# A graph attention layer's edge stage: queries two chunks ahead, values turned and copied first, row loads on another queue

## The reference, cut to what matters

```python
q = (embeds[rows] @ qW).reshape(e, HEADS, dh)          # rows = src, HEADS = 4, dh = 24
k = (embeds[cols] @ kW).reshape(e, HEADS, dh)          # cols = dst
v = (embeds[cols] @ vW).reshape(e, HEADS, dh)
scores = jnp.clip(jnp.einsum('ehd,ehd->eh', q, k), -10.0, 10.0)
exp_s = jnp.exp(scores)
norms = jax.ops.segment_sum(exp_s, rows, num_segments=nvar)[rows]
w = exp_s / (norms + 1e-08)
res = jax.ops.segment_sum(w[:, :, None] * v, rows, num_segments=nvar).reshape(nvar, d)
```

## Time and profile before

| | |
|---|---|
| median of 3 runs | 12264.51 us (12244.3 to 12269.51) |
| profiled execution, its own time | 12250.97 us |
| its span, first to last instruction | 12249.1 us |
| TensorE busy | 8795.0 us (72%) |
| VectorE busy | 5775.9 us (47%) |
| ScalarE busy | 2582.4 us (21%) |
| GpSimd busy | 8413.7 us (69%) |
| transfers | 1189.05 MB, mean 97 GB/s |

### The profile page before, as it was taken

The page is one execution under the profiler, slowest core; times in us unless marked ns, Lnnn a source line. Parts: engine busy times, 40 slices in busy tenths (PEclk is TensorE's granted clock), DMA queues, the critical chain, the costliest instruction groups (busy, mean ns, idle before and its releaser), DMA issues. The chain is left out here.

```text
span 12249.1 us, 129981 instructions
## 1 busy us (share of the span) xinstructions
PE 8795.0 (72%) x34411; PEld 6536.1 (53%) x34411; DVE 5775.9 (47%) x10781; ACT 2582.4 (21%) x5194; POOL 8413.7 (69%) x8582
## 2 busy tenths in 40 slices
PE   2136777776679999987999999799999925445452
PEld 2125555555556666655666666566666623333331
DVE  4975555555543333334333333333333345555555
ACT  0001111111112222221222222122222213333332
POOL 1047767766777777764777777677777757777776
PEclk9655555555555555555555555555555555555555
DMA  3036666666533333332333333233333313333332
GB/s 99 0 105 155 153 152 154 153 154 152 138 86 93 94 93 93 94 80 56 93 93 93 94 93 94 74 93 94 93 93 94 93 44 82 81 82 82 81 81 49
DMA packets 1017000, 1189.05 MB, mean 97 GB/s; under 512 B 481524, under 2 KB 834195, under 8 KB 1015919
## 3 DMA queue, kind: packets, MB, share of 16 engines
q0 software_dynamic: 305536, 521.41, 19.7%
q1 hardware_dynamic: 697975, 654.50, 17.3%
q10 hardware_dynamic: 12768, 4.82, 0.1%
HBM read 751.68 MB, written 428.15 MB: 96 GB/s over the span
## 5 line engine op out<-in xcount | busy, mean ns | idle before, releaser
L837 POOL DMA_INDIRECT e_got<-kv_tab,dst_cols x1664 | 1846.5, 1110 | 677.5 <-issue 467.3
L1050 POOL DMA_INDIRECT e2a_got<-x_tab,e2a_idx x1616 | 1524.9, 944 | 616.2 <-issue 492.2
L1678 POOL DMA_INDIRECT e_got<-h_tab,e_idx x1616 | 1526.5, 945 | 536.3 <-issue 454.9
L1050 POOL DMA_INDIRECT e2b_got<-x_tab,e2b_idx x1616 | 1524.7, 944 | 508.3 <-issue 492.2
L1050 POOL DMA_INDIRECT e_got<-x_tab,e_idx x1616 | 1524.8, 944 | 506.5 <-issue 492.1
L847 PE MATMUL e_Q<-e_window,e_pick 128*128 128x96 f32 x3328 | 829.1, 431 | 842.3 <-issue 747.1
L847 PEld LDWEIGHTS e_Q<-e_window,e_pick 128*128 128x128 f32 x3328 | 741.0, 328 | 958.4 <-issue 956.2
L1070 PE MATMUL e_EA<-we_We,e_attr 33*128 33x96 f32 x3232 | 879.8, 451 | 88.5 <-DMA e_attr<-in_attr_T 88.5
L1070 PE MATMUL e2a_EA<-we_W_edge,e2a_attr 33*128 33x96 f32 x3232 | 879.8, 451 | 3.4 <-DMA e2a_attr<-in_attr_T 3.4
L1070 PE MATMUL e2b_EA<-we_W_edge,e2b_attr 33*128 33x96 f32 x3232 | 879.8, 451 | 3.4 <-DMA e2b_attr<-in_attr_T 3.4
L1070 PEld LDWEIGHTS e_EA<-we_We,e_attr 33*128 33x128 f32 x3232 | 783.0, 324 | 179.2 <-issue 90.2
(11 more groups left out here) (348 smaller groups left out, 15816.9 us busy)
## 6 DMA issues: line engine op xcount, KB each, us to landing
scan_out<-e_out SPq DMA_DIRECT2D x416, 200.0 KB, 2.2
e_window<-q_tab SPq DMA_DIRECT2D x1664, 48.0 KB
scan_out<-e_out SPq DMA_DIRECT2D x404, 194.0 KB, 2.2
scan_out<-e_out SPq DMA_DIRECT2D x404, 192.0 KB, 2.2
scan_out<-e2a_out SPq DMA_DIRECT2D x404, 192.0 KB, 2.2
scan_out<-e2b_out SPq DMA_DIRECT2D x404, 192.0 KB, 2.2
e_rel<-rel_row SPq DMA_DIRECT2D x416, 128.0 KB
e_attr<-in_attr_T SPq DMA_DIRECT2D x404, 66.0 KB
```

Source lines behind the costliest of these rows:

```text
L837: e.indirect_dma_start(got[u][:, k, :], None, kv_tab, bass.IndirectOffsetOnAxis(dst_c[:, c * K + k:c * K + k + 1], axis=0)).then_inc(s_g[u ...
L1050: e.indirect_dma_start(got[u][:, k, :], None, x_tab, bass.IndirectOffsetOnAxis(idx[u][:, k:k + 1], axis=0)).then_inc(s_g[u], 16)
L1678: e.indirect_dma_start(got[u][:, k, :], None, h_tab, bass.IndirectOffsetOnAxis(idx[u][:, k:k + 1], axis=0)).then_inc(s_g[u], 16)
```

## The change

Three moves, all inside the edge stage of the attention layer.

- `queries` and `picks`: two chunks are made before the loop, and step c makes those of c+2 instead of c+1. TensorE makes them at the end of its step, after the turn-back, instead of at its start. VectorE's place for `picks` stays the same.
- ScalarE copies the turned values of chunk c (L933) before it copies out the sums of chunk c-1 (L922).
- The loads of `rel` and `keep` go from SyncE's list into a new function `rows_in` in ScalarE's: those of the first four chunks before its loop, those of c+4 at the end of step c, with the same two waits. SyncE keeps the windows and the stores.

```diff
--- before.py
+++ after.py
@@ -813,14 +813,10 @@
 
                     for c in range(NCH0):
                         u = c % U
-                        after(e, v_pick, c - U + 1)
-                        e.dma_start(rel[u][:, :], rel_c[c:c + 1].to_broadcast([P, CH])).then_inc(s_rel[u], 16)
                         after(e, t_q, c - U + 1)
                         for k in range(K):
                             row = e.value_load(first_row[0:1, c * K + k:c * K + k + 1], min_val=0, max_val=TROW - P)
                             e.dma_start(window[u][:, k, :], q_tab[bass.ds(row, P), :]).then_inc(s_w[u], 16)
-                        after(e, t_z, c - U + 1)
-                        e.dma_start(keep[u][:, :], keep_c[c:c + 1]).then_inc(s_keep[u], 16)
                         if c >= U:
                             store(c - U)
                     for c in range(NCH0 - U, NCH0):
@@ -855,9 +851,8 @@
                         ins.then_inc(t_back, 1)
 
                     queries(0)
+                    queries(1)
                     for c in range(NCH0):
-                        if c + 1 < NCH0:
-                            queries(c + 1)
                         e.wait_ge(s_keep[c % U], 16 * (c // U + 1))
                         after(e, v_scan, c - 1)
                         e.matmul(Z[c % 2][0:PAY, :], ones_b[:, 0:PAY], keep[c % U][:, :], start=True, stop=True).then_inc(t_z, 1)
@@ -868,6 +863,8 @@
                         ins.then_inc(t_fwd, 1)
                         if c > 0:
                             turn_back(c - 1)
+                        if c + 2 < NCH0:
+                            queries(c + 2)
                     turn_back(NCH0 - 1)
 
                 @block.vector
@@ -889,6 +886,7 @@
                     e.memset(run[1][:, :], 0.0).then_inc(s_init, 1)
                     e.wait_ge(s_init, 1)
                     picks(0)
+                    picks(1)
                     for c in range(NCH0):
                         s = c % 2
                         e.wait_ge(s_g[c % U], 16 * K * (c // U + 1))
@@ -903,8 +901,8 @@
                         e.scalar_tensor_tensor(score[s][:, :, :], score[s][:, :, :], -10.0,
                                                top_score[:, c * K:(c + 1) * K].unsqueeze(2).to_broadcast([P, K, HEADS]),
                                                ALU.max, ALU.min).then_inc(v_clip, 1)
-                        if c + 1 < NCH0:
-                            picks(c + 1)
+                        if c + 2 < NCH0:
+                            picks(c + 2)
                         if c > 0:
                             scan(c - 1)
                         e.wait_ge(a_exp, c + 1)
@@ -921,16 +919,26 @@
                             e.wait_ge(s_st[c % U], 16 * (c // U))
                         e.activation(out[c % U][:, :, :], B[c % 2][:, 0:K * PAY].rearrange("p (k d) -> p k d", k=K), ACT.Copy).then_inc(a_out, 1)
 
+                    def rows_in(c):
+                        after(e, v_pick, c - U + 1)
+                        e.dma_start(rel[c % U][:, :], rel_c[c:c + 1].to_broadcast([P, CH])).then_inc(s_rel[c % U], 16)
+                        after(e, t_z, c - U + 1)
+                        e.dma_start(keep[c % U][:, :], keep_c[c:c + 1]).then_inc(s_keep[c % U], 16)
+
+                    for c in range(U):
+                        rows_in(c)
                     for c in range(NCH0):
                         s = c % 2
                         e.wait_ge(v_clip, c + 1)
                         after(e, t_fwd, c - 1)
                         e.activation(pay[s][:, :, D:PAY], score[s][:, :, :], ACT.Exp).then_inc(a_exp, 1)
-                        if c > 0:
-                            to_out(c - 1)
                         e.wait_ge(t_fwd, c + 1)
                         after(e, v_scan, c - 1)
                         e.activation(msg[s][:, :], M[s][0:PAY, :], ACT.Copy).then_inc(a_msg, 1)
+                        if c > 0:
+                            to_out(c - 1)
+                        if c + U < NCH0:
+                            rows_in(c + U)
                     to_out(NCH0 - 1)
```

## The result

The changed kernel takes 12175.59 us (12172.78 to 12186.14, 4 runs) where the kernel before takes 12260.64 (12244.3 to 12269.51): a ratio of 0.9934, interval 0.9917 to 0.9951. It is faster by 85 us; 376 were forecast, and 12176 lies outside the range of 11810 to 12060. The profiled execution took 12175.47 us, span 12173.6. From the first gather's start to the last one's the stage runs 2450.9 us against 2516.9 before, so it gives 66 of the 75.5 us by which the spans differ.

The account below looks back on a forecast made before the run. SyncE's issue of seven transfers was taken as the bound; its cycle falling from 6.083 to 5.17 us over 412 chunks saves 376 us, the other parts 0, so 12264.5 becomes 11888 us, range 11810 to 12060.

Parts of the forecast that it names:

- SyncE's seven issues: Edge stage, claimed bound before the change: SyncE issues seven transfers per chunk end to end, mean cycle 6.083 us.
- rule against this: Skill page's rule on row loads: spreading transfers over issuing engines saves only small initiation time; gain about 0, 12264 us.
- GpSimd is next, at its measured price: Rival: edge-stage gathers at 1110 ns plus issue, 5.56 us per chunk, bind next; gain 214 us, 12050; chance 0.10.
- the wait for the weighting, once booked inside the gather: Argument against the GpSimd rival: a 1.65 us fourth gather and a 1.12 us later start are waiting, not service.
- The counterexample: Following gather group, cited against the GpSimd rival: short fourth gather, next gather 0.27 us after the weighting's end.
- SyncE's cycle: SyncE's time per edge-stage chunk without rel and keep: from 6.083 to 5.17 us, between 5.10 and 5.25.
- the register load: SyncE's load for the window address: store to first window 1.28 to 1.43 us, against rel to window 1.51.
- ScalarE's two issues: rel and keep on ScalarE's queue: 0.42 + 0.32 us plus gaps, 0.85 per chunk, hidden under SyncE's cycle.
- The swap of the copies: ScalarE copies turned values before the copy-out: scan about 1.0 us earlier, worth nothing; bounds 0.1 us per chunk either way.
- two-chunk lead: Queries and picks made two chunks ahead: worth 0 while SyncE sets the pace, bounds -0.1 to +0.1 us per chunk.

Follow-up runs that it names:

- e1: Kernel before with only the rel and keep loads moved to ScalarE's queue, old order kept: 12184.75 us, ratio 0.9925.
- e6b: Kernel before with only the weighting's weights read from PSUM, repeated on a chip of usual speed: 12260.24 us, ratio 1.0002.
- e3: Changed kernel with a second exp, into PSUM, from where the weighting reads its weights: 11851.31 us, ratio 0.9656.
- e10: Kernel of e3 plus a VectorE product of two SBUF operands directly behind the scan: 14196.55 us, kernel before 14244 on that chip.
- e7b: Kernel before with weights in PSUM and row loads on ScalarE's queue, old order, repeated on a chip of usual speed: 11828.0 us, ratio 0.9648.
- e2: Changed kernel with rel and keep loads back on SyncE, so only the order differs from the kernel before: 12235.72 us, ratio 0.9969.
- e4: Changed kernel plus one VectorE product of two SBUF operands behind the product of keys and queries: 12324.6 us, ratio 1.0041.
- e5b: Changed kernel plus one VectorE product with one PSUM operand behind the key-query product, repeated on a chip of usual speed: 12263.78 us, ratio 1.0003.
- e11b: Changed kernel with VectorE's pick moved between scan and weighting, repeated on a chip of usual speed: 12296.37 us, ratio 1.0027.
- e9: Kernel of e3 plus a VectorE product of two SBUF operands behind the key-query product: 14406.39 us, kernel before 14244 on that chip.
- e3b: Kernel of e3 run again, on a chip where the kernel before took 14244 us: 14426.68 us.

## Why the prediction was wrong

*What bounded the kernel before* was right: SyncE's seven issues (e1 and e6b). The prediction's *rule against this*, by which the move gives about 0, is answered by e1: 12271.44 - 12184.75 = 87 us from the queue alone.

*The step that failed* is the rejection of the rival "GpSimd is next, at its measured price", which left GpSimd at 5.00 us per chunk, under SyncE's 5.17; it takes 5.9. The prediction took the gather of 1.65 us and the next one's start 1.12 us after the weighting's end as "the wait for the weighting, once booked inside the gather". It was service: the gather was held while the weighting ran and took another 0.82 us after it, and the 0.3 us of issue made up the 1.12. The counterexample, 0.27 us after the end, was a gather that had ended 0.23 us before the weighting started, so that nothing was held. The trace of before could have told: of the 221 gathers there that have a weighting in their first 945 ns 220 are long. Nor does the next stage, with its 944 ns, speak against it: its product (L1122) has one operand in PSUM, and it has no operation like the weighting.

*The rival was also too cheap.* It gave 5.56 us per chunk from a mean in which 163 of the 416 weightings held no gather: before the change GpSimd often waited for the weighting (206.7 us). Once GpSimd never waits, 411 of 416 hold one and the mean goes to 1169 ns: 5.9 us, 12176 instead of 12050. So GpSimd's own pace stood only 0.2 us under SyncE's 6.083, and the rest of what SyncE was relieved of bought nothing.

*The hold itself.* The Trainium skill, page "SBUF — State Buffer", section "SBUF: two separate sides", names a VectorE operation "with two SBUF inputs" among those that take the port shared with GpSimd, though only against a GpSimd operation that reads SBUF, and says that the one that comes second fully blocks. The gather takes its row numbers from SBUF, so it may count as such; no run separates that. The prediction gave this rival 0.10. e3 agrees with the section: one operand moved to PSUM, and 1169 ns become 964. By that section whichever starts first keeps the port; the held gathers behind a scan had started up to 1.1 us before the operation (e10), so there the measurement decides otherwise.

*SyncE's cycle* was forecast at 5.17 us, 5.10 at the least. From store to windows it now takes a median 1.09 us, so with 3.6 of windows it would be some 4.8 (an estimate from these two), and GpSimd's 5.05 binds in e7b. The term at fault is the register load: it takes a mean 0.65 us with `rel` in front and 0.28 behind the store alone, 0.37 less, where the prediction took off 0.15 at most. Mis-sized, but without weight in the result.

*ScalarE's two issues* cost 0.33 and 0.30, forecast 0.42 and 0.32, and were hidden. *The swap of the copies* works as said: the copy starts at 2010.20, 0.04 us after the turn's end. With the two-chunk lead it is worth 36 us while SyncE binds (e2), where 0 with bounds of 0.1 us per chunk for each of the two was given; -0.09 us lies inside.

*One sum holds for all kernels that GpSimd binds.* The difference of the gathers' mean from 1169 ns, times 4 x 416, against the time beyond 12176 us: e3 -341 against -324, e7b -353 against -348, e4 +140 against +149, e5b +82 against +88, e11b +113 against +121. Only e1 fits less well, +27 against +9; its profiled execution was its slowest, 34 us above its median.

## What to carry to other kernels

A mean that is too high for its kind of instruction (1110 ns against 944 a stage later) has to be explained before its neighbour's wait is called the reason: list what the other engines do during the long ones and during the short. When the queue in front of a bound is relieved, price the next engine at what it costs when it never waits, since its waits had hidden its holds. Where gathers issued by GpSimd bind, try to give VectorE's two-operand products one operand in PSUM, above all directly behind a scan: here 2.7% on top of the moved queue (e3), and nothing without it (e6b).

## What the runs showed of the hardware

- A gather of GpSimd that is caught by a VectorE product of two SBUF operands ends 0.82 us after that product's end, whenever it started. Undisturbed it takes 0.945 us, so it seems to stand still some 0.12 us after its start (an estimate from these two). With one operand in PSUM it isn't held (e3).
- Directly behind a 1.28 us scan such an operation also holds gathers that started up to 1.05 to 1.1 us before its own start (e10), behind a 0.56 us product only those that start while it runs (e9).
- The pick, 512 values from bf16 to f32 with one SBUF operand of that size, holds the 176 gathers of e3 that started 0.09 to 0.34 us after its start in the same way, until 0.82 us after its end. 15 that started 0.36 to 0.47 us before it end 0.12 us after its end, which the products with two SBUF operands show nowhere.
- SyncE's load of a register from memory takes 0.27 us behind a window's transfer and 0.28 behind the 200 KB store alone (changed kernel). In the kernel before it takes 0.46 behind the 128 KB row load (before the first store) and 0.65 once the store stands in front of the row load.
- Two of the four chips of the experiments took 14244 to 14262 us for the kernel before, and one of these took 14405.61 for the changed kernel: ratio 1.011 (1.0093 to 1.0127), slower. In its trace the edge stages are longer (this one by 338 us, the other four by 410 to 489), while the sort and the gathers of the node stages take as long as in the trace shown above. Now and then SyncE stands still between two issues. These are four windows in the changed kernel on such a chip; 3.6 us is usual:

```profile
2016.65 5.77 SPq L819 DMA_DIRECT2D e_window<-q_tab  x4
```

From 900 to 4000 us GpSimd waits 718.6 us there for the weighting and TensorE's queries 985.1 us for something unseen. The gathers' mean is 960 ns, where 1170 was expected: the weighting holds 41 of them, for 12 us in all, so e3b, at 14426.68, had little to gain. e10, with held gathers, is even faster there (0.996 and 0.9946). What slows those chips, and why the changed kernel loses on one of them, stays open.
